# The router of a batch, three to four steps of the attention order earlier

## The reference

```
x = layernorm(x + attention(x))          # 16 heads of 16, causal, softmax
scores = x @ gate_w.T                    # 16 experts
probs  = softmax(scores)
idx    = top_k(probs + gate_b, 6)
y      = sum over the 6 chosen experts of probs[e] * expert_e(x)
z      = shared expert(x)
out    = layernorm(x + y + z)
```

## Time and profile before

| | |
|---|---|
| median of three runs | 1070.45 us (1070.27 to 1071.28) |
| profiled execution, its own time | 1073.4 us |
| its span | 1071.6 us |
| PE busy | 993.2 us (93%) |
| DVE busy | 811.9 us (76%) |
| POOL busy | 752.0 us (70%) |
| ACT busy | 734.7 us (69%) |
| the chain that ended last | PE 71%, DVE 16%, ACT 5%, issue 4% |

### The profile page before, as it was taken

How to read it: one execution, slowest core, us unless ns; L and a number is a source line. 1 busy time by engine, 2 the same in 40 slices (tenths; PEclk the granted TensorE clock), 3 DMA queues, 4 the chain that set the end, 5 groups by cost and what they waited for, 6 DMA issues and landing times.

```text
span 1071.6 us, 27815 instructions
## 1 busy us (share of the span) xinstructions
PE 993.2 (93%) x7534; PEld 791.1 (74%) x7535; DVE 811.9 (76%) x2622; ACT 734.7 (69%) x1859; POOL 752.0 (70%) x677
## 2 busy tenths in 40 slices
PE   7899999999999998899899999999999999999982
PEld 4545555656565554459889999999999999999871
DVE  8776878888888888848767687777777777777496
ACT  4577566676666665667455598878888888888545
POOL 4224548888888888877754677777777777777576
PEclk8899999999999999999899999999999999999986
DMA  6633244555555555367778988878877878788793
GB/s 183 174 113 101 85 139 153 180 163 172 161 174 171 168 167 188 124 209 222 251 227 199 214 153 159 135 129 133 131 131 130 134 130 134 131 136 175 191 385 130
DMA packets 136716, 176.37 MB, mean 165 GB/s; under 512 B 19584, under 2 KB 113840, under 8 KB 136368
## 3 DMA queue, kind: packets, MB, share of 16 engines
q1 hardware_dynamic: 88016, 105.83, 33.4%
q0 software_dynamic: 39024, 54.29, 28.7%
q10 hardware_dynamic: 9584, 15.11, 4.7%
HBM read 73.68 MB, written 78.17 MB: 142 GB/s over the span
## 4 chain that ended last, share of the span: by engine, by line
PE 71%; DVE 16%; ACT 5%; issue 4%; DMA 1%; POOL 1%; SPq 1%; ACTq 0%; POOLq 0%; DVEq 0%
PE psum L1118 19%; PE psum L840 11%; PE psum L1145 7%; PE psum L885 5%; PE psum L1148 4%; PE psum L873 4%; DVE rowmax L1629 4%; PE psum L854 4%; PE psum L1101 4%; PE psum L1131 2%; ACT probs L1243 2%; PE psum L1132 2%; PE psum L1082 2%; PE psum L860 1%; PE psum L917 1%
## 5 line engine op out<-in xcount | busy, mean ns | idle before, releaser
L1243 ACT ACTIVATE probs<-psum 128x512 f32<-128x512 f32 (+2 forms) x384 | 186.5, 530 | 118.8 <-PE psum L873 116.7
L1629 DVE TENSOR_REDUCE rowmax<-psum 128x1 f32<-128x512 f32 (+3 forms) x352 | 212.1, 633 | 54.3 <-PE psum L860 52.0
L2188 POOL DMA_INDIRECT xs_d<-x1p,index x192 | 204.1, 1063 | 54.3 <-issue 39.4
L1118 PE MATMUL psum<-we_hi_lo,xb_hi 128*128 x828 | 206.7, 332 | 0.0
L1976 DVE TENSOR_TENSOR hb<-psum,hb 128x176 f32<-128x176 f32 x207 | 70.7, 342 | 96.7 <-ACT hb L1424 90.8
L2260 POOL DMA_INDIRECT x_d<-y_sb,tokens x69 | 108.5, 1572 | 49.5 <-issue 28.6
L2100 POOL TENSOR_SCALAR_AFFINE_SELECT probs<-probs 128x512 f32<-128x512 f32 x128 | 87.3, 682 | 78.6 <-ACT probs L1243 76.3
L1118 PEld LDWEIGHTS psum<-we_hi_lo,xb_hi 128*128 128x128 f32 x828 | 136.9, 188 | 2.9 <-issue 0.2
L854 PE MATMUL psum<-stack_k,stack_q 96*128 96x256 bf16 (+3 forms) x512 | 129.1, 310 | 7.6 <-DMA stack_k<-k_l 2.4
L2260 POOL DMA_INDIRECT z_d<-y_sb,tokens x69 | 108.6, 1573 | 38.2 <-issue 25.3
L1118 PE MATMUL psum<-we_hi_lo,xb_lo 128*128 x414 | 133.6, 323 | 0.0
(11 more groups left out here) (227 smaller groups left out, 2553.9 us busy)
## 6 DMA issues: line engine op xcount, KB each, us to landing
xb<-xs_d SPq DMA_DIRECT2D x207, 138.0 KB
stack_q<-q_h SPq DMA_DIRECT2D x48, 128.0 KB
stack_k<-k_h SPq DMA_DIRECT2D x45, 128.0 KB
w_raw<-in_we SPq DMA_DIRECT2D x9, 608.0 KB, 4.4
xT_raw<-in_xT SPq DMA_DIRECT2D x9, 512.0 KB, 4.5
stack_q<-q_m SPq DMA_DIRECT2D x32, 128.0 KB
stack_k<-k_m SPq DMA_DIRECT2D x32, 128.0 KB
x_res<-in_x SPq DMA_DIRECT2D x8, 512.0 KB, 4.2
```

The costliest lines, as they stand in the source:

```text
L1118: last = nc.tensor.matmul(uv, (xb_hi, xb_lo)[a][k % 2][:, d, :], w_flat[:, bass.ds(at + b * W_COLS + d * UP, UP)], start=False, stop=d == ...
L1243: nc.scalar.activation(probs[kt][:, heads[0]:heads[0] + n, :], st[f % ST_BANKS][:, 0:n * width].rearrange("p (h t) -> p h t", h=n), ACT.Ex ...
L1629: nc.vector.reduce_max(rowmax[gpar][:, heads[0]:heads[0] + n, qt], src, AX.X).then_inc(sm_free, 1)
L2188: nc.gpsimd.indirect_dma_start(out=xs_d[:, :], out_offset=bass.IndirectOffsetOnAxis(ap=index[tp][:, n:n + 1], axis=0), in_=x1p[tp][:, n // ...
```

## The change

Three tables change, and nothing else. The stage `r` goes from (3, 1) to (2, 7) on PE. The softmax on ACT goes from (3, 2) to (3, 0). The five parts on DVE go from (3, 1), (3, 2), (3, 4), (3, 5), (3, 6) to (2, 7), (3, 0), (3, 2), (3, 3), (3, 5). No instruction is added or removed, and the lists of POOL and SP are as they were. The epilogue, in which the last batch's router runs, is the same too; so the change acts seven times, in the bodies of batches 1 to 7.

```
 MISC = {
...
-    (2, 1): "m", (2, 4): "x0", (2, 5): "x1",
-    (3, 0): "m", (3, 1): "r", (3, 7): "d",
+    (2, 1): "m", (2, 4): "x0", (2, 5): "x1", (2, 7): "r",
+    (3, 0): "m", (3, 7): "d",
 }
...
-ROUTE_AT = {(3, 1): 0, (3, 2): 1, (3, 4): 2, (3, 5): 3, (3, 6): 4}
-SOFTMAX_AT = (3, 2)
+ROUTE_AT = {(2, 7): 0, (3, 0): 1, (3, 2): 2, (3, 3): 3, (3, 5): 4}
+SOFTMAX_AT = (3, 0)
```

## The result

The change takes 1099.95 us (median of four runs, 1094.94 to 1106.02), against 1070.87 us before (1070.27 to 1072.39): a ratio of 1.0283, 95% interval 1.0256 to 1.0311. It is slower, by some 29 us where 17.8 us were forecast, and outside the range. The profiled execution is the fastest of the four, 1094.94 us with a span of 1093.2 us. Its granted clock was 0.969 over the span, and the four runs had 0.969, 0.969, 0.959 and 0.955, in the order of their times 1094.94, 1095.99, 1103.90 and 1106.02 us. The kernel before had 0.977 in its profile.

A forecast was written before the change was run, and what follows sets the result against it. PE, busy in 93% of the span, bounds the kernel, with DVE last in the fourth quarter. Five bodies at 2.75 us (13.8), batch 1 at 3.2 and batch 7 at 0.9 add 17.8 us to 1070.45: 1088.2 us, range 1080 to 1094.

The forecast's parts named there:

- PE's wait for `t_lo`: At (2, 7), ahead of the moved router, PE stands still until POOL ends `t_lo`: 1.04 us of new idle time.
- ACT at (3, 2): PE waits for ACT to free score banks at the P of (3, 2): 0.84 us, then about 0.3 us.
- DVE up to L1706: From the first row maximum of (3, 0) DVE needs 10.63 us, so L1706 ends 2.86 us later.
- its soft part: Two-input DVE operations beside POOL vary by contention: +/-0.4 us a body at one such instruction.
- PE at L1706: At (3, 7) PE waits for DVE to read the attention: some 1.9 us in place of 0.99 us.
- The body: One attention body becomes 2.75 us longer, bounds 1.04 to 3.5 us, with nothing given back in the next.
- the step on the clock: TensorE's clock across the new waits: no time for a fall was put into the sum.
- its rival: New waits let TensorE's clock fall for a third of each quarter, some 4 us a body: 1116 us, 2 in 100.
- The early router: Router out of the way at (3, 1) to (3, 6), closing PE's idle times: 11.6 us faster, 1058.9 us, 3 in 100.
- came back: PE's 1.04 us are taken up by the 1.65 us of idle time behind: 1070.5 us, 4 in 100.
- PE and ACT alone: L1706 on DVE isn't last; PE and ACT give 1.9 us a body: 1083.2 us, 18 in 100.
- waits for POOL's masks: POOL's masks, from (3, 1) on, come after PE's need, one more microsecond a body: 1095 us, 7 in 100.

The follow-up runs named there:

- only the wait: The kernel before, with only PE's wait for `t_lo` put at (2, 7) and the router left at (3, 1): 1078.32 us, ratio 1.0065.
- the filled runs: The change with PE's three longest new waits of a body filled by matmuls of ones: median 1090.09 us, ratio 1.0171; its fastest two runs are meant.

## Why the prediction was wrong

It named a time 12 us too low. Of its steps, those on the order held:

- *PE's wait for `t_lo`:* 1.04 us forecast, 1.05 us measured in batches 2 to 6, 1.46 us in batch 1 (1.46 us forecast) and 1.60 us in batch 7 (1.58 us forecast); by itself it costs 1.0 us a body (only the wait).
- *ACT at (3, 2):* 0.84 and 0.3 us forecast, 0.74 and 0.15 us measured. The wait for the logits was 0.34 us, against 0.40 us.
- *DVE up to L1706:* 10.63 us forecast from its first row maximum, 369.43 to 379.98 = 10.55 us measured; 3 us of waiting at (2, 7) forecast, 3.28 us measured. That the length agrees is in part luck. The short wait at the second row maxima of (3, 2) was put at 0.10 us and was 0.65 us, and two small operations that the sum took over as they were (the kind that the prediction calls its soft part) got shorter by about as much (0.70 to 0.27 us and 0.45 to 0.20 us); before, then in the change:

```profile
409.03 0.70 DVE L1687 TENSOR_TENSOR shift_rest<-shift,shift_h 16x128 f32<-16x128 f32 x1
410.30 0.45 DVE L1690 CAST shift_m<-shift_rest 16x128 bf16<-16x128 f32 x1
```

```profile
371.02 0.27 DVE L1687 TENSOR_TENSOR shift_rest<-shift,shift_h 16x128 f32<-16x128 f32 x1
371.91 0.20 DVE L1690 CAST shift_m<-shift_rest 16x128 bf16<-16x128 f32 x1
```

- *PE at L1706:* its wait was 1.33 us and not 1.9 us, but 0.70 us came up ahead, at `rowmax`, which no step had: together 2.0 us.
- *The body:* 2.75 us forecast. From where PE gets to the router's place to the first work of the next body it is 2.72 us more (365.50 to 381.25 against 406.79 to 419.82). Then 0.25 us come back in the next body, in which I had expected nothing back: 58.39 against 55.9 us, 2.47 us. They come back at once, at `m` of (0, 0) (L905), which needs row maxima of DVE. Before, these stood behind the router's part 4; in the change part 4 is done ahead of L1706, and L905 follows the P by 0.43 in place of 0.67 us. Before, then in the change:

```profile
364.19 0.59 PE L873 MATMUL psum<-stack_q,stack_k 99*128 99x512 bf16 x2
364.86 0.27 PE L905 MATMUL psum<-ident,rowmax 128*16 128x128 f32 x1
```

```profile
381.53 0.59 PE L873 MATMUL psum<-stack_q,stack_k 99*128 99x512 bf16 x2
381.96 0.28 PE L905 MATMUL psum<-ident,rowmax 128*16 128x128 f32 x1
```

At the clock of the kernel before, the change would by estimate take about what the forecast says: the line through its runs, drawn out from 0.969, is at 1087 us for 0.98, the filled runs with that clock took 1087.01 and 1088.73 us, and the forecast was 1088.2 us.

What failed is the step on the clock: the sum put it at nothing, and its rival was given 2 in 100 and left out of the range. By the line through the runs it cost 12.7 us in all (1099.95 - 1087.2, an estimate), 1.8 us a body on average. The rival's size of 4 us a body doesn't follow from its own words: a third of a 14 us quarter at half the clock loses at most 2.3 us, and of four quarters 9.3 us. The argument against it was that idle times of 0.66 and 0.99 us had passed at a granted clock of 1.00, so that one of 1.04 us should. (For the 1.9 us at L1706, twice the old wait, even that was no argument.) It weighed the length of a wait and not what is next to it. In the earlier trace rows A and dense scores stand behind each wait (but for 0.24 us of `d` behind the second), and the router's 1.8 us of sparse matmuls stand amid dense ones. The change put the two side by side. The Trainium skill, page TensorE: Matmul & The Clock Gate, section Part 1 on what is actually happening, says that activity releases the throttle. The trace agrees so far: the clock fell where idle time and narrow matmuls stood together, in each of seven bodies, and not where 512-column ones stood in their place. PE's busy time doesn't show that difference, since it is without a gap over the 16-column matmuls too. By that rule the rival deserved more than 2 in 100.

What stays open: why the same wait and router let the clock fall in some bodies and not in others, also of one run (248 us, but not 368 us); why it fell once behind the router with only 0.08 us of wait; why three dense matmuls among the router's didn't help; and what makes the stretches at L1706 or, in the experiments, at other waits.

The other rivals fell. The early router didn't fill PE's idle time. Nothing but 0.25 us came back. PE and ACT alone don't set the body in the change: it got 0.8 us shorter with DVE's split out of the way. Of waits for POOL's masks PE shows none of over 0.15 us in the profile's bodies.

## What to carry to other kernels

When an instruction is moved up on an engine, look first at what its operand needs and when that was ready: the wait it brings along was hidden under the work that it is moved past, and so was the time that another engine used there. Then look at what will stand next to the new wait on TensorE. An idle time and a stage of narrow matmuls, each harmless in the trace, can together let the clock fall, and then the time spreads from run to run with the mean clock; a few dense matmuls on constants in the wait are a cheap test of that (here 8 to 10 us of the 29 us). And when a sum agrees with the trace, compare its terms too: two of them were off here, by 0.55 and 0.68 us in opposite directions.

## What the runs showed of the hardware

- The clock fell in seven of seven bodies behind a wait of 0.96 us with 16 matmuls of 16 and 32 columns behind it, and in none behind one of 0.97 us with 8 matmuls of 512 columns (1.73 us), with all else the same: 1112.67 against 1089.51 us. The 16 without the wait: none, 1082.38 us.
- Runs of one program differed by up to 11 us (1.0%), close to a line with their mean granted clock: 7.8 us for 0.01, over clocks of 0.955 to 0.969.
- A stretch of 3 to 4 us at 1.2 GHz behind the router cost 0.9 us of a body, one at the wait for L1706 1.6 us, and one of some 7 us behind the router 2.4 us: each less than half its length.
